# A GRU, attention, RK4 and FFN kernel: other stages for the FFN's side work on ScalarE and VectorE

## The chip, the cores and the metric

One core of a Trainium2 chip runs the whole program. The metric is the device time of one execution in microseconds: 1735.76 us before the change, the median of 3 runs (1735.63 to 1736.38).

## What is computed

Cut to what matters (x is 32 x 64 x 512, fp32):

```python
x = x + attn(gru(cond, x))                 # over 32 sequences of 64 steps
# the state q of the RK4 recurrence, 64 steps of 4 stages
def derivative(q, p, drive):
    dq = q - q ** 3 / 3.0 - p + drive + tanh(q) @ coupling.T + bias
    dp = EPSILON * (q + ALPHA - BETA * p)
    return dq, dp
# one step: dq1..dq4 from q, q + 0.5*DT*dq1, q + 0.5*DT*dq2, q + DT*dq3; then clip
# the FFN on every q, quantized to fp8 (scales per row from the row's maximum):
qx = fp8(xr / (max|xr| / 448))
g = qlinear(qx, w_gate); u = qlinear(qx, w_up)      # 512 -> 1408
t = silu(g) * u
y = qlinear(fp8(t / (max|t| / 448)), w_down)        # 1408 -> 512
out = x + y
```

The derivatives of a step follow each other: each stage needs the tanh of the state that the stage before it left. The FFN only reads the states.

## The kernel before

The program runs three parts one after the other: the GRU with the preparation of the FFN's weights, the attention, and the RK4 recurrence with the FFN. The change lies in the third, which takes the last 650 us or so. Every engine runs a program of its own, in order, and waits on semaphores.

**Groups and stages.** 64 time steps make 16 groups of 4 steps; a group has 16 stages, numbered k = 0 to 15 (k // 4 is the step, k % 4 the stage `st` of the RK4 step). Groups 0 to 2 and 15 are written out, groups 3 to 14 are the 12 turns of a loop (`in_groups`). A tile of the FFN is the 128 rows that a group of 4 steps has produced. Its work takes the three groups that follow: in group g, `tile(0)` is tile g-1, `tile(1)` is g-2 and `tile(2)` is g-3. After group 15 three groups without stages (16 to 18) finish the tiles that are left.

**One stage, engine by engine** (`stage` of each engine). DVE computes the new state with L1317 (from PSUM, where PE has summed) and turns it with two transposes (L1275). ACT squares the state (L956, into PSUM) and takes the tanh in two halves (L964), in stages with `st` = 0 the tanh first; then it weighs it for the p sum (L959). PE multiplies the tanh by the coupling in 32 products (L775) and mixes in the states for the next stage (L765). DVE meanwhile computes `ebuf` from the square (L1308), seeds the bank of the next stage (L1296, or L1294 after stages with `st` = 3), and then runs `fill()`, which is the FFN's slot of that stage, before it waits for PE and computes the next state. POOL adds the parts of p (`p_step`, L514 to L524) and then runs its own slot.

**The slots.** `slot(k, ...)` of PE, ACT, DVE and POOL place the FFN's work behind the stage k of its engine. On DVE before the change: the maximum of x (L1341, 512 wide) in k = 5 and its scale and reciprocal (L1346, L1347) in 6; x's exponents (L1350, L1351) in 7; `gate_part` (L1414) in 12, 13, 0 and 2; `gated_part` (L1422) in 14, 1, 4 and 5; the maximum of t in two halves of 704 (L1365) in 3 and 6, and its reciprocal (L1369 to L1371) in 7; t's exponents `t_bits` (L1395: 768 wide in 8, 640 in 9); `t_grid` (L1401) in 9 and 10; `t_added` (L1407) in 11 and 15; y's scaling (L1389) in 10. On ACT: Silu (`silu_part`, L978) in 12, 13, 0 and 2, the scaling of x (L1002) in 6, of t (`t_scaled`, L985) in 7 and 8, copies of transposed t (`t_kept`, L992) in 1 and 4, of x (L1005) in 10. On POOL, which the change doesn't touch: x's rounding (L543 in 7, L548 in 8), `gate_scaled` (L529) in 13, 14, 1 and 3, `t_rounded` (L536) in 12 and 15, and the output's sum (L563) in 11.

**The drive sum.** `drive_sum` (L1285) adds the drive of the next time step and the bias, both in SBUF, into PSUM. It stands behind `fill()` in the stages with `st` = 2, so in k = 2, 6, 10 and 14:

```python
                fill()
                if st == 2 and not end:
                    drive_sum(t + 1, (s + 1) % 4, g + 1 + (s == 3))
                dve.wait_ge(rk_e, n + 1)
                dve.wait_ge(rk_mm, n + 1)
```

Of the kernel before, what the change touches and what calls it, by code (L numbers as in the profile page):

```python
# [5 lines left out]
ALU = mybir.AluOpType  # L6
# [79 lines left out]
GROUP_STEPS = 12  # L86
# [51 lines left out]
def gru_attn_rk4_ffn(nc, xT, x, cond_quad, cond_T, W_ih, W_hh, bias_ih, bias_hh, sel, gamma, Wq, Wkv, Wo,  # L138
                     couplingT, bias_quad, w_gate, w_up, w_down, down_idx, ident, mean_of, trig, mask,
                     x1_scr, q_scr, wgu_scr, wd_scr, scale_scr, out):  # L140
    with ExitStack() as ctx:
# [123 lines left out]
        tam2 = f32(w.take(2), 2)  # L265
        tam, tsx, tsy, trs, xam, xsx, xrs = (f32(w.take(1), 1) for _ in range(7))
# [590 lines left out]
        def _(act):  # L857
# [137 lines left out]
            def slot(k, tile):  # L995
                i = tile(0)
                if i is not None:
                    if k == 6:
                        act.wait_ge(f_rq, i + 1)

                        wait_if(act, f_q8, i)
                        act.activation(vq, qt, ACT.Copy, scale=xrs).then_inc(f_vq, 1)  # L1002
                    if k == 10:
                        act.wait_ge(f_qT, i + 1)
                        act.activation(qxT, ps[:, 6, 0:2 * P].bitcast(BF16).rearrange("p (c n) -> p c n", c=NC), ACT.Copy).then_inc(f_qTcp, 1)  # L1005
                    if k in (12, 13):
                        silu_part(i, k - 12)
                i = tile(1)
                if i is not None:
                    if k in (0, 2):  # L1010
                        silu_part(i, 2 + k // 2)
                    if k in (7, 8):
                        t_scaled(i, k - 7)
                i = tile(2)
                if i is not None:
                    if k == 1:
                        t_kept(i, 0)
                    if k == 4:
                        t_kept(i, 1)

            act.wait_ge(ct_ld, 16 * 4)
            act.wait_ge(rk_bits, 1)
# [10 lines left out]
        def _(dve):  # L1033
# [267 lines left out]
            def stage(g, s, st, last, fill):  # L1301
# [10 lines left out]
                if st == 2 and not end:  # L1312
                    drive_sum(t + 1, (s + 1) % 4, g + 1 + (s == 3))
# [18 lines left out]
            def slot(v, k, tile):  # L1332
# [5 lines left out]
                if i is not None:  # L1338
                    if k == 5:
                        dve.wait_ge(q_ld, 16 * TILE_T * (i + 1))  # L1340
                        v.did(dve.tensor_reduce(xam, qt, AX.X, ALU.max, apply_absolute_value=True))  # L1341
                    if k == 6:
                        v.need(v.n)
                        if tile(1) is not None:
                            dve.wait_ge(f_gated, GU_T * tile(1) + GU_T)
                        v.need(v.did(dve.tensor_scalar(xsx, xam, 1.0 / FP8_MAX, None, ALU.mult)))  # L1346
                        dve.reciprocal(xrs, xsx).then_inc(f_rq, 1)  # L1347
                    if k == 7:
                        dve.wait_ge(f_vq, PRIMED + i + 1)
                        v.need(v.did(dve.tensor_scalar(eq.bitcast(U32), vq.bitcast(U32), EXP_BITS, None, ALU.bitwise_and)))  # L1350
                        dve.tensor_scalar(eq, eq, FP8_TINY, ROUND_AT, ALU.max, ALU.mult).then_inc(f_xe, 1)  # L1351
                    if k in (12, 13):
                        gate_part(i, k - 12)
# [3 lines left out]
                if i is not None:  # L1357
# [4 lines left out]
                    if k in (3, 6):  # L1362
                        half = k // 6
                        dve.wait_ge(f_gated, GU_T * i + 2 * half + 2)
                        v.did(dve.tensor_reduce(tam2[:, half:half + 1], tt[:, half * 2 * GU_N:(half + 1) * 2 * GU_N], AX.X, ALU.max,  # L1365
                                                apply_absolute_value=True))
                    if k == 7:
                        v.need(v.n)
                        v.need(v.did(dve.tensor_reduce(tam, tam2, AX.X, ALU.max)))  # L1369
# [148 lines left out]
```

## Time and profile before

| | us |
|---|---|
| median of 3 runs (lowest, highest) | 1735.76 (1735.63, 1736.38) |
| the profiled execution, its own time | 1733.82 |
| its span in the profile | 1732.0 |
| PE busy (matmuls) | 1551.0 (90%) |
| DVE busy | 1126.0 (65%) |
| ACT busy | 507.8 (29%) |
| POOL busy | 380.3 (22%) |
| first and last state update L1317 | 1079.8 and 1686.1 |

Times in the profile are counted from the span's start. In the timeline a row is one instruction (or a few alike in a row), with its start and its length; in brackets stands how long its engine had been idle before it and which instruction released it. A row without brackets followed its engine's earlier work directly. An engine starts an instruction a little before the one ahead of it has ended. `mem` is SBUF and `ps` is PSUM, so `ps<-mem` is an instruction whose inputs are all in SBUF and whose output is in PSUM.

### The profile page before, as it was taken

Reading aid. Unit: us, or ns where it says so; the run is one execution under the profiler, and the core shown is the slowest. Engines: PE = TensorE matmul, PEld = TensorE weight load, DVE = VectorE, ACT = ScalarE, POOL = GpSimd, SP = SyncE. Lnnn points to the kernel's source line nnn. Section 1 sums busy time; section 2 is a strip of 40 time slices with the busy share of each in tenths; the row PEclk is TensorE's granted clock in tenths of the full one; section 3 lists DMA queues with packets and bytes.
Section 4 is the critical chain, followed back from the end, with each engine's and each line's share of the span. In section 5 each row is a group of like instructions: output and inputs, shape, how many; then the busy total and the mean of one; then the engine's idle time right before and its main releaser. Section 6 shows DMA issues by size and latency. Waiting matters only on the chain.

```text
span 1732.0 us, 45724 instructions
## 1 busy us (share of the span) xinstructions
PE 1551.0 (90%) x16744; PEld 951.5 (55%) x16744; DVE 1126.0 (65%) x3319; ACT 507.8 (29%) x1589; POOL 380.3 (22%) x554
## 2 busy tenths in 40 slices
PE   5999899999859999999999998788888888888884
PEld 2333333333738576675767753556666666666662
DVE  2888743333786475664747541568888888888885
ACT  1233211112120202102020110355555555555552
POOL 1222010000000000000000000235555555555554
PEclk9999999999969999999999998999999999999997
DMA  7322210005000000000000005101111111111111
GB/s 303 79 76 61 79 29 12 12 11 111 1 0 1 25 0 24 6 18 23 1 24 0 24 6 184 42 23 29 33 31 44 35 35 33 30 33 30 42 35 35
DMA packets 88432, 70.27 MB, mean 41 GB/s; under 512 B 30728, under 2 KB 80824, under 8 KB 87352
## 3 DMA queue, kind: packets, MB, share of 16 engines
q1 hardware_dynamic: 86616, 63.75, 12.7%
q0 software_dynamic: 1760, 5.77, 1.2%
q8 instruction: 35, 0.57, 0.1%
q14 instruction: 21, 0.17, 0.0%
HBM read 52.55 MB, written 16.92 MB: 40 GB/s over the span
## 4 chain that ended last, share of the span: by engine, by line
PE 69%; DVE 14%; issue 8%; ACT 5%; DMA 2%; POOL 1%; SPq 1%; ACTq 0%; DVEq 0%; POOLq 0%
PE ps L681 13%; PE ps L671 13%; PE ps L775 10%; PE ps L588 9%; PE ps L596 9%; PE ps L715 3%; PE ps L765 2%; PE ps L739 2%; ACT mem L964 2%; DVE mem L1317 2%; DVE mem L1275 2%; ACT ps L956 2%; PE ps L692 1%; PE ps L789 1%; PE ps L585 1%
## 5 line engine op out<-in xcount | busy, mean ns | idle before, releaser
L775 PE MATMUL ps<-mem 128*32 128x128 f32 x8192 | 280.7, 278 | 89.7 <-ACT mem L964 85.6
L775 PEld LDWEIGHTS ps<-mem 128*32 128x32 f32 x8192 | 212.8, 111 | 165.2 <-ACT mem L964 118.3
L671 PE MATMUL ps<-mem 128*128 128x512 f32 x512 | 224.6, 593 | 0.0
L681 PE MATMUL ps<-mem 128*128 128x256 f32 x1024 | 222.3, 379 | 0.0
L681 PEld LDWEIGHTS ps<-mem 128*128 128x128 f32 x1024 | 194.2, 190 | 25.8
L514 POOL TENSOR_TENSOR mem<-mem 128x128 f32<-128x128 f32 x64 | 30.7, 480 | 784.7 <-ACT mem L959 784.5
L588 PE MATMUL ps<-mem 128*32 128x384 f32 x2048 | 181.5, 496 | 0.0
L596 PE MATMUL ps<-mem 128*32 128x384 f32 x2048 | 179.0, 491 | 2.7 <-DVE mem L1122 2.7
L671 PEld LDWEIGHTS ps<-mem 128*128 128x128 f32 x512 | 95.7, 190 | 109.6 <-issue 109.2
L518 POOL TENSOR_TENSOR mem<-mem 128x128 f32<-128x128 f32 x192 | 101.2, 527 | 171.8 <-ACT mem L959 165.7
L765 PE MATMUL ps<-mem 128*128 128x128 f32 x768 | 138.6, 304 | 0.0
L964 ACT ACTIVATE mem<-mem 128x64 f32<-128x64 f32 x512 | 102.0, 246 | 111.6 <-DVE mem L1275 111.6
L931 ACT ACTIVATE mem<-mem 128x512 f32<-128x512 f32 x32 | 19.7, 630 | 391.3 <-DVE mem L1216 391.3
L596 PEld LDWEIGHTS ps<-mem 128*32 128x32 f32 x2048 | 67.0, 111 | 103.1 <-issue 87.0
L765 PEld LDWEIGHTS ps<-mem 128*128 128x128 f32 x768 | 101.5, 192 | 38.8 <-issue 26.7
L1108 DVE TENSOR_TENSOR mem<-mem,ps 128x128 f32<-128x128 f32 x64 | 18.4, 287 | 158.9 <-ACT mem L860 158.8
L1179 DVE TENSOR_TENSOR mem<-ps,mem 64x256 f32<-64x256 f32 x272 | 114.7, 422 | 8.4
L588 PEld LDWEIGHTS ps<-mem 128*32 128x32 f32 x2048 | 60.7, 111 | 90.3 <-issue 90.3
L956 ACT ACTIVATE ps<-mem 128x128 f32<-128x128 f32 x256 | 71.0, 277 | 125.6 <-DVE mem L1317 119.6
L1308 DVE SCALAR_TENSOR_TENSOR mem<-ps,mem 128x128 f32<-128x128 f32 x256 | 74.5, 291 | 42.8 <-ACT ps L956 42.3
L789 PE MATMUL ps<-mem 128*128 128x352 bf16 x512 | 98.8, 318 | 2.7 <-DVE mem L1422 1.1
L1177 DVE TENSOR_TENSOR mem<-ps,mem 128x256 f32<-128x256 f32 x136 | 57.7, 425 | 66.9 <-PE ps L692 37.1
(129 smaller groups left out, 2104.8 us busy)
## 6 DMA issues: line engine op xcount, KB each, us to landing
mem<-x_scr SPq DMA_DIRECT2D x128, 64.0 KB, 1.8
mem<-in_xT SPq DMA_DIRECT2D x64, 64.0 KB, 1.8
mem<-in_Wq SPq DMA_DIRECT2D x1, 4096.0 KB
mem<-in_Wo SPq DMA_DIRECT2D x1, 4096.0 KB
mem<-in_x SPq DMA_DIRECT2D x16, 256.0 KB, 2.7
x_scr<-mem SPq DMA_DIRECT2D x32, 128.0 KB, 2.3
q_scr<-mem SPq DMA_DIRECT2D x64, 64.0 KB, 1.6
mem<-q_scr SPq DMA_DIRECT2D x64, 64.0 KB, 1.9
```

What stands on the lines that cost most here:

```text
L518: tt(pacc, pacc, pw[1 + st], ALU.add).then_inc(rk_pa, 1)
L588: mm = pe.matmul(ps[32 * j:32 * j + 32, par, 0:3 * P].rearrange("p (g n) -> p g n", g=3), xt[par][:, c, :], wih[:, c, :].rearrange("p (g j ...
L596: mm = pe.matmul(ps[32 * j:32 * j + 32, par, P:4 * P].rearrange("p (g n) -> p g n", g=3), hT[1 - par][:, c, :], whh[:, c, :].rearrange("p ...
L671: mm = pe.matmul(ps[:, 6 + pr, :], aoT[:, h, pr * P:pr * P + P], wo[:, h, :], start=(h == 0), stop=(h == HEADS - 1))
L681: mm = pe.matmul(ps[:, h % Q_BANKS, 0:BLK], wq[:, c, h * DH:(h + 1) * DH], xnb[:, c, :], start=(c == 0), stop=(c == NC - 1))
L765: pe.matmul(ps[:, st % 2, 0:P], mix[m], (None, qn[(s - 1) % 4], *qst)[k], start=False, stop=False, skip_group_check=True)
L775: mm = pe.matmul(ps[32 * j:32 * j + 32, st % 2, 0:P], thT[:, c, :], ct[:, c, j * P:(j + 1) * P], start=False, stop=(c == NC - 1), skip_gro ...
L789: mm = pe.matmul(ps[:, 2 + order % 2, 0:GU_N], qxT[:, c, :], (wgT if gate else wuT)[:, c, m * GU_N:(m + 1) * GU_N], start=(c == 0), stop=( ...
L956: act.activation(ps[:, 5, 0:P], src, ACT.Square, scale=(STEP[st] / 3) ** 0.5).then_inc(rk_sq, 1)
L964: act.activation(thT[:, 2 * half:2 * half + 2, :], qsT[:, 2 * half:2 * half + 2, :], ACT.Tanh).then_inc(rk_th, 1)
L1179: dve.tensor_tensor(share[b:b + DH // 2], src[a:a + DH // 2], bcast(trigs[:, tr + 1, :], BLK_B)[a:a + DH // 2], ALU.mult).then_inc(done, 1)
L1308: stt(out=ebuf, in0=ps[:, 5, 0:P], scalar=KEPT[st], in1=qs, op0=ALU.subtract, op1=ALU.mult).then_inc(rk_e, 1)
```

## The change

Nothing is computed otherwise, except that t's maximum is taken in four parts in place of two, and a copy of x's scale is added. In the stages of a group:

- ACT: Silu goes from k = 12, 13, 0, 2 to 13, 14, 1, 3; x's scaling from 6 to 4; the copies of transposed t from 1 and 4 to 0 and 5.
- DVE: x's maximum, scale and reciprocal go to k = 3, the scale into `xnew`, which is copied to `xsx` in 8. t's maximum is taken in parts of 352 in k = 1, 2, 5 and 6, and its reciprocal goes from 7 to 6.
- DVE: the drive sum goes from the stages with `st` = 2 to those with `st` = 0, so from k = 2, 6, 10, 14 to 0, 4, 8, 12.
- ACT: two waits ahead of the first group are dropped; DVE gets one wait on its own earlier work in k = 12.

```diff
--- before.py
+++ after.py
@@ -83,7 +83,7 @@
 GU_SLOTS = (11, 12, 13, 15, 0, 1, 3, 4)
 DOWN_SLOTS = (5, 7, 8, 9)
 T_PARTS = ((0, 6 * P), (6 * P, INNER))
-GROUP_STEPS = 12
+GROUP_STEPS = 15
 
 
 def wait_if(eng, sem, value):
@@ -262,8 +262,8 @@
         t8T = bf16(w.take(INNER // 2), IC, P)
         ysc = f32(w.take(D), D)
         yout = f32(w.take(D), D)
-        tam2 = f32(w.take(2), 2)
-        tam, tsx, tsy, trs, xam, xsx, xrs = (f32(w.take(1), 1) for _ in range(7))
+        tam4 = f32(w.take(4), 4)
+        tam, tsx, tsy, trs, xam, xnew, xsx, xrs = (f32(w.take(1), 1) for _ in range(8))
 
         (wih_ld, whh_ld, w_att, b_ld, c_ld, xt_ld0, xt_ld1, h0_ld, st_ld, wg_ld, wu_ld, idx_ld, wd_ld, x_ld, x1_wr, q_ld, x1_ld,
          o_wr, ct_ld) = (sem(n) for n in (
@@ -995,7 +995,7 @@
             def slot(k, tile):
                 i = tile(0)
                 if i is not None:
-                    if k == 6:
+                    if k == 4:
                         act.wait_ge(f_rq, i + 1)
 
                         wait_if(act, f_q8, i)
@@ -1003,23 +1003,20 @@
                     if k == 10:
                         act.wait_ge(f_qT, i + 1)
                         act.activation(qxT, ps[:, 6, 0:2 * P].bitcast(BF16).rearrange("p (c n) -> p c n", c=NC), ACT.Copy).then_inc(f_qTcp, 1)
-                    if k in (12, 13):
-                        silu_part(i, k - 12)
+                    if k in (13, 14):
+                        silu_part(i, k - 13)
                 i = tile(1)
                 if i is not None:
-                    if k in (0, 2):
+                    if k in (1, 3):
                         silu_part(i, 2 + k // 2)
                     if k in (7, 8):
                         t_scaled(i, k - 7)
                 i = tile(2)
                 if i is not None:
-                    if k == 1:
+                    if k == 0:
                         t_kept(i, 0)
-                    if k == 4:
+                    if k == 5:
                         t_kept(i, 1)
-
-            act.wait_ge(ct_ld, 16 * 4)
-            act.wait_ge(rk_bits, 1)
 
             def group(g, rk, tile):
                 for k in range(16):
@@ -1309,7 +1306,7 @@
                 if st < 3:
                     seed(t, s, st + 1)
                 fill()
-                if st == 2 and not end:
+                if st == 0 and not (last and s == 3):
                     drive_sum(t + 1, (s + 1) % 4, g + 1 + (s == 3))
                 dve.wait_ge(rk_e, n + 1)
                 dve.wait_ge(rk_mm, n + 1)
@@ -1336,20 +1333,22 @@
                     v.did(dve.tensor_copy(tsy, tsx))
                 i = tile(0)
                 if i is not None:
-                    if k == 5:
+                    if k == 3:
                         dve.wait_ge(q_ld, 16 * TILE_T * (i + 1))
-                        v.did(dve.tensor_reduce(xam, qt, AX.X, ALU.max, apply_absolute_value=True))
-                    if k == 6:
-                        v.need(v.n)
-                        if tile(1) is not None:
-                            dve.wait_ge(f_gated, GU_T * tile(1) + GU_T)
-                        v.need(v.did(dve.tensor_scalar(xsx, xam, 1.0 / FP8_MAX, None, ALU.mult)))
-                        dve.reciprocal(xrs, xsx).then_inc(f_rq, 1)
+                        v.need(v.did(dve.tensor_reduce(xam, qt, AX.X, ALU.max, apply_absolute_value=True)))
+                        v.need(v.did(dve.tensor_scalar(xnew, xam, 1.0 / FP8_MAX, None, ALU.mult)))
+                        dve.reciprocal(xrs, xnew).then_inc(f_rq, 1)
                     if k == 7:
                         dve.wait_ge(f_vq, PRIMED + i + 1)
                         v.need(v.did(dve.tensor_scalar(eq.bitcast(U32), vq.bitcast(U32), EXP_BITS, None, ALU.bitwise_and)))
                         dve.tensor_scalar(eq, eq, FP8_TINY, ROUND_AT, ALU.max, ALU.mult).then_inc(f_xe, 1)
+                    if k == 8:
+                        if tile(1) is not None:
+                            dve.wait_ge(f_gated, GU_T * tile(1) + GU_T)
+                        v.did(dve.tensor_copy(xsx, xnew))
                     if k in (12, 13):
+                        if k == 12:
+                            v.need(v.n)
                         gate_part(i, k - 12)
                     if k == 14:
                         gated_part(i, 0)
@@ -1359,14 +1358,13 @@
                         gate_part(i, 2 + k // 2)
                     if k in (1, 4, 5):
                         gated_part(i, {1: 1, 4: 2, 5: 3}[k])
-                    if k in (3, 6):
-                        half = k // 6
-                        dve.wait_ge(f_gated, GU_T * i + 2 * half + 2)
-                        v.did(dve.tensor_reduce(tam2[:, half:half + 1], tt[:, half * 2 * GU_N:(half + 1) * 2 * GU_N], AX.X, ALU.max,
-                                                apply_absolute_value=True))
-                    if k == 7:
+                    if k in (1, 2, 5, 6):
+                        m = (1, 2, 5, 6).index(k)
+                        dve.wait_ge(f_gated, GU_T * i + m + 1)
+                        v.did(dve.tensor_reduce(tam4[:, m:m + 1], tt[:, m * GU_N:(m + 1) * GU_N], AX.X, ALU.max, apply_absolute_value=True))
+                    if k == 6:
                         v.need(v.n)
-                        v.need(v.did(dve.tensor_reduce(tam, tam2, AX.X, ALU.max)))
+                        v.need(v.did(dve.tensor_reduce(tam, tam4, AX.X, ALU.max)))
                         v.need(v.did(dve.tensor_scalar(tsx, tam, 1.0 / FP8_MAX, None, ALU.mult)))
                         dve.reciprocal(trs, tsx).then_inc(f_rt, 1)
                     if k == 8:
```

PE's and POOL's instructions stand in the same order as before; only line numbers differ. Two places on DVE, both inside the loop over groups 3 to 14. The lines are shifted there: L1317 is L1314 in the changed kernel, L1308 is L1305, L1296 is L1293, L1285 is L1282, L1395 is L1393, L1414 is L1412.

The stage k = 8, before (from `ebuf` to the new state; ISA and REGISTER_ALU rows compute the values of later waits):

```order
L1308 SCALAR_TENSOR_TENSOR mem<-ps,mem 128x128 [waits rk_sq]
L1296 SCALAR_TENSOR_TENSOR ps<-mem,ps 128x128
L1394 ISA
L1395 TENSOR_SCALAR mem<-mem 128x768 [waits f_vt]
L1317 SCALAR_TENSOR_TENSOR mem<-ps,mem 128x128 [waits rk_mm,rk_e]
```

and with the change (L1348 is the copy of x's scale):

```order
L1305 SCALAR_TENSOR_TENSOR mem<-ps,mem 128x128 [waits rk_sq]
L1293 SCALAR_TENSOR_TENSOR ps<-mem,ps 128x128
L1348 COPY mem<-mem 128x1 [waits f_gated]
L1392 ISA
L1393 TENSOR_SCALAR mem<-mem 128x768 [waits f_vt]
L1282 TENSOR_TENSOR ps<-mem 128x128 [waits drive_ld3]
L1314 SCALAR_TENSOR_TENSOR mem<-ps,mem 128x128 [waits rk_mm,rk_e]
```

Two instructions are new there: the copy ahead of `t_bits`, and the drive sum behind it, ahead of the new state.

The stage k = 12, before (L1414 is `gate_part`):

```order
L1308 SCALAR_TENSOR_TENSOR mem<-ps,mem 128x128 [waits rk_sq]
L1296 SCALAR_TENSOR_TENSOR ps<-mem,ps 128x128
L1411 ISA
L92 REGISTER_ALU [waits f_g]
L1414 SCALAR_TENSOR_TENSOR mem<-ps,mem 128x352 [waits f_sig]
L1317 SCALAR_TENSOR_TENSOR mem<-ps,mem 128x128 [waits rk_mm,rk_e]
```

and with the change:

```order
L1305 SCALAR_TENSOR_TENSOR mem<-ps,mem 128x128 [waits rk_sq]
L1293 SCALAR_TENSOR_TENSOR ps<-mem,ps 128x128
L1409 ISA [waits rk_v]
L92 REGISTER_ALU [waits f_g]
L1412 SCALAR_TENSOR_TENSOR mem<-ps,mem 128x352 [waits f_sig]
L1281 ISA
L1282 TENSOR_TENSOR ps<-mem 128x128 [waits drive_ld0]
L1314 SCALAR_TENSOR_TENSOR mem<-ps,mem 128x128 [waits rk_mm,rk_e]
```

The drive sum now stands between `gate_part` and the new state. The stages 0 and 4 get it at the same place.

## Rows read from the trace of the kernel before

**Rows 1.** The page, part 4: the chain that ended last, by engine
```profile
PE 69%; DVE 14%; issue 8%; ACT 5%; DMA 2%; POOL 1%; SPq 1%; ACTq 0%; DVEq 0%; POOLq 0%
```

**Rows 2.** Timeline, DVE, stages 2 and 3: start, length, engine, line, operation
```profile
1312.50 0.29 DVE L1317 SCALAR_TENSOR_TENSOR mem<-ps,mem 128x128 f32<-128x128 f32 x1 [0.27 <-PE ps L775]
1313.35 0.88 DVE L1365 TENSOR_REDUCE mem<-mem 128x1 f32<-128x704 f32 x1
1314.63 0.30 DVE L1317 SCALAR_TENSOR_TENSOR ps<-ps,mem 128x128 f32<-128x128 f32 x1 [0.41 <-PE ps L775]
```

**Rows 3.** Timeline, DVE, ACT and POOL, stages 7 and 8
```profile
1323.54 0.30 DVE L1317 SCALAR_TENSOR_TENSOR ps<-ps,mem 128x128 f32<-128x128 f32 x1
...
1323.70 0.94 ACT L985 ACTIVATE mem<-mem 128x768 f32<-128x768 f32 x1 [1.08 <-DVE mem L1371]
...
1324.04 1.27 POOL L543 TENSOR_TENSOR mem<-mem 128x512 f32<-128x512 f32 x1
...
1325.47 1.27 POOL L548 TENSOR_TENSOR mem<-mem 128x512 bf16<-128x512 f32 x1 [0.16 <-POOL mem L543]
...
1325.53 1.63 DVE L1395 TENSOR_SCALAR mem<-mem 128x768 uint32<-128x768 uint32 x1
...
1327.08 0.28 DVE L1317 SCALAR_TENSOR_TENSOR mem<-ps,mem 128x128 f32<-128x128 f32 x1
```

**Rows 4.** Timeline, DVE and SP, from stage 15 into stage 0
```profile
1305.62 0.30 DVE L1317 SCALAR_TENSOR_TENSOR ps<-ps,mem 128x128 f32<-128x128 f32 x1 [0.47 <-PE ps L775]
...
1307.45 0.58 DVE L1414 SCALAR_TENSOR_TENSOR mem<-ps,mem 128x352 f32<-128x352 f32 x1
...
1308.04 1.75 SPq L435 DMA_DIRECT2D mem<-q_scr  x4
```

**Rows 5.** Timeline, DVE, ACT and POOL, stages 11 to 13
```profile
1334.56 0.30 DVE L1317 SCALAR_TENSOR_TENSOR ps<-ps,mem 128x128 f32<-128x128 f32 x1 [0.25 <-PE ps L775]
...
1336.45 1.82 POOL L536 TENSOR_TENSOR mem<-mem 128x768 bf16<-128x768 f32 x1
...
1336.48 0.58 DVE L1414 SCALAR_TENSOR_TENSOR mem<-ps,mem 128x352 f32<-128x352 f32 x1
...
1336.97 0.28 DVE L1317 SCALAR_TENSOR_TENSOR mem<-ps,mem 128x128 f32<-128x128 f32 x1
...
1337.17 0.50 ACT L978 ACTIVATE mem<-mem 128x352 f32<-128x352 f32 x1 [0.90 <-DVE mem L1414]
...
1339.29 0.29 DVE L1317 SCALAR_TENSOR_TENSOR mem<-ps,mem 128x128 f32<-128x128 f32 x1 [0.44 <-PE ps L775]
```

**Rows 6.** Timeline, DVE and POOL: two places with the drive sum L1285
```profile
1178.15 0.56 POOL L518 TENSOR_TENSOR mem<-mem 128x128 f32<-128x128 f32 x1 [0.93 <-ACT mem L959]
...
1178.32 0.55 DVE L1285 TENSOR_TENSOR ps<-mem 128x128 f32<-128x128 f32 x1
...
1331.46 0.29 DVE L1285 TENSOR_TENSOR ps<-mem 128x128 f32<-128x128 f32 x1
...
1331.66 0.28 DVE L1317 SCALAR_TENSOR_TENSOR mem<-ps,mem 128x128 f32<-128x128 f32 x1
```

**Rows 7.** Timeline, DVE and POOL, after the last stage
```profile
1715.30 2.75 DVE L1407 TENSOR_TENSOR mem<-mem 128x768 f32<-128x768 f32 x2
...
1715.46 1.90 POOL L563 TENSOR_TENSOR mem<-mem 128x512 f32<-128x512 f32 x1 [6.39 <-DVE mem L1389]
```

**Rows 8.** Timeline, DVE and POOL, stage 7 in groups 2 and 6
```profile
1170.65 0.46 POOL L518 TENSOR_TENSOR mem<-mem 128x128 f32<-128x128 f32 x1 [1.82 <-ACT mem L959]
...
1170.66 0.73 DVE L1351 TENSOR_SCALAR mem<-mem 128x512 f32<-128x512 f32 x1
...
1322.71 0.43 DVE L1351 TENSOR_SCALAR mem<-mem 128x512 f32<-128x512 f32 x1
...
1322.77 0.68 POOL L518 TENSOR_TENSOR mem<-mem 128x128 f32<-128x128 f32 x1 [1.82 <-ACT mem L959]
```

**Rows 9.** Timeline, DVE, after the last stage: the loads of the last tile
```profile
1690.66 0.69 DVE L1341 TENSOR_REDUCE mem<-mem 128x1 f32<-128x512 f32 x1 [0.45 <-DMA mem<-q_scr]
```

## The prediction

> **What bounds the kernel now.** I read four views: the chain that ended last, the timeline of each engine through one turn of the loop, the timelines of places where DVE and POOL meet, and the end behind the last stage. The change touches the RK4 part alone, and there a stage costs what lies between two state updates L1317. The shortest are 2.13 us: from 1312.50 to 1314.63 in [rows 2], where DVE did a maximum of 0.88 us on the side and still waited 0.41 us for PE. So side work is free as long as it fits behind DVE's own part. PE has 69% of the chain [rows 1], mostly as a link of this ring (tanh, product, update, transpose). Two of the stages that the change touches are longer because something ends late.
>
> From stage 7 to 8 it is 3.54 us (1323.54 to 1327.08) [rows 3]. ACT's scaling of t starts only at 1323.70, when its reciprocal is there, and keeps ACT from the tanh. And t's exponents L1395, 768 wide, take 1.63 us: they start 0.06 us behind POOL's L548, which lasts 1.27 us, and end 0.42 us after it. DVE and POOL hold each other up here.
>
> From 11 to 12 it is 2.41 us and from 12 to 13 2.32 us [rows 5]. In stage 12 `gate_part` ends what DVE has to do and L1317 follows without idle time; then Silu (1337.17 to 1337.67) keeps ACT from the square of the new state.
>
> **Who holds whom.** Rows 6 to 8 are about instructions of DVE that read two SBUF operands, or read and write wide ones in SBUF, beside POOL's. The drive sum takes 0.29 us alone and the next instruction starts 0.20 us after it [rows 6]. Where POOL's L518 was under way until 1178.71, it took 0.55 and ended at 1178.87, so 0.16 behind POOL. Behind the last stage [rows 7] two L1407 stand back to back; POOL's L563 starts 0.16 us after the first, takes 1.90 in place of the 1.27 of sums of its size [rows 3], and the second L1407 ends 0.68 us after L563. So a waiting POOL gets its turn between two DVE instructions, and the second one waits for all of POOL's. In [rows 8] L1351 starts 0.01 us behind POOL's L518 and takes 0.73; where it starts 0.06 ahead it takes 0.43 and L518 pays (0.68).
>
> **The change, per turn of the loop** (12 turns, groups 3 to 14):
>
> 1. Silu one stage later: it starts right behind ACT's own work and is over before the next state. The stages 12 and 0 lose what is above the floor: 2.32 less some 2.15, -0.17 each, -0.34 (bounds 0, if something else ends as late, and -0.38 by the 2.13 of [rows 2]). In 13, 14, 1 and 3 a Silu of 0.50 us lies in ACT's idle time.
> 2. The drive sum in stages 0, 4 and 12: DVE has no idle time ahead of L1317 there, and behind `gate_part` or `gated_part` the sum adds its 0.20 us to each. Stages 0 and 4: +0.40.
> 3. In stage 12 it meets POOL's `t_rounded`. The sum would start at 1336.97 and run into L536, which holds POOL from 1336.45 to 1338.27 [rows 5]. By [rows 6] it ends 0.16 behind it, at 1338.43, and L1317 starts 0.09 before that end (0.20 after the start of a 0.29 one), at 1338.34 in place of 1336.97: **+1.36**. L536 doesn't move, since POOL's row of work ahead of it is the same. Bounds: +0.20 if the sum isn't held, +1.45 if L1317 waits for its end.
> 4. The drive sum leaves 2, 6, 10 and 14. In 2 and 14 it was hidden. In 10 L1317 comes 0.20 earlier (1331.46 to 1331.66), but the tanh behind it waits for ACT's copy of x, which hangs on PE: 0. In 6 L1317 gets back to PE's pace: -0.03.
> 5. Maxima: 0.88 us for 704 [rows 2] and 0.69 for 512 [rows 9] make some 0.5 for 352, an estimate. In 1, 2 and 5 this fits ahead of the update by 0.1 us or more, in 6 with the three small ones (0.15 to 0.16 us each, 0.19 apart) by 0.2. x's maximum in 3 takes the place of t's, with two small ones behind it. It needs the tile's loads 4.4 us earlier than in 5; their last is issued by 1309.8 [rows 4] and stage 3's slot starts at 1313.35 [rows 2]: hidden. All 0. Should 1 or 5 miss by 0.05, a turn costs 0.1 more.
> 6. Reciprocal of t in 6, so ACT scales t (0.94) right behind its own work of stage 7, beside PE's product, and is done before the new state of 1323.54; the tanh comes in time. x's scaling in 4 and the copies of t in 0 and 5 lie in ACT's idle time in the same way: 0, and 0.1 each if one should reach the next square. The start of L1395 moves from 1.99 behind L1317 (1323.54 to 1325.53) to 1.84 as in stage 0 [rows 4], plus 0.06 for the copy ahead: 1.90. POOL's L548 stays at 1.93 behind, with L543 over at 1.77 [rows 3]. **L1395 is first by 0.03 us.** It then runs its 0.56, and L548 gets POOL's turn behind it and ends at some 3.59. But the drive sum is the next on DVE, and as the second L1407 of [rows 7] it waits for L548: end 3.74, L1317 at 3.65 in place of 3.54. +0.11. If L548 is first, L1395 ends where it did and the sum adds +0.20. The gain of this move (L1317 at 2.58, so -0.96) is there only if the sum slips in behind L1395.
>
> Sum of a turn: -0.34 + 0.40 + 1.36 - 0.03 + 0.11 = **+1.50**, times 12 is +18.0. Group 1: its stage 8 has no L1395, but the sum meets L548 (+0.6). Group 2: about +0.5, since L536 is over in time there. Group 15: +1.6, as a turn. Together +2.7. Behind the last stage DVE waits for the last tile's loads until 1690.66 [rows 9]; two gated parts and t's maxima of the tile before stand behind this wait now, and the last tile's chain starts about 1 us later, of which a shorter queue later gives back some: +0.8, between -0.4 and +2. In all **+21.5** on 1733.82, the profiled execution's own time (1.8 above its span); the median of the runs stands 1.9 above it, so 1735.76 + 21.5 = **1757.3 us**, 1.2% slower.
>
> Which of the two is first in stage 8 is worth 0.09 a turn. The rows leave it open: POOL wins from 0.01 ahead, DVE from 0.06 ahead, and 0.03 lies between. [...]
>
> **Rivals.**
> - *The sum slips in behind L1395* before POOL takes its turn: stage 8 gives 1.07 less, a turn +0.43, the whole 12 x 0.43 + 2.7 + 0.8 = +8.7, 1744.5 us. For it: L1395 is another instruction than L1407, and the next one starts 0.08 before it ends. Against it: [rows 7]. 7 in 100.
> - *Faster: the drive sum isn't held by L548 and L536.* Then stage 12 costs 0.20 and stage 8 gives 0.96: -0.34 + 0.60 - 0.03 - 0.96 = -0.73 a turn, -8.8 for the loop; with groups 1, 2 and 15 (+1.0) and the end (+0.8) -7.0, 1728.8 us. It decides at stage 12: with stage 8's 0.96 won, the change pays from where the sum costs less than about 0.8 there. Against it speak the 0.55 us and [rows 7]; for it only that no row shows the sum beside L536. 7 in 100.
> - *Held at stage 8 alone*: 1.16 less a turn than forecast, and as much in group 15: some +6.4, 1742.2 us. 4 in 100.
> - *Little happens*: ACT and DVE have more room than the rows show and the parts cancel, within 0.2%. 4 in 100.
>
> **The numbers.** The forecast has 78 in 100. Its own range is 1754.5 to 1761: 0.05 a turn at stage 12, 0.1 at stages 1 and 5, 1.1 for the lost lead, -1.2 to +1.2 for the end. To leave out no more than 2 in 10 the range reaches to the first rival: 1744 to 1762. A change of 0.2% (3.5 us) is about what a measurement of this kernel can tell from none. Faster by more 7 in 100, within it 4, slower 89.
>
> **What would show it.** In the changed profile the drive sum of stage 12 (L1282) lasts about 1.45 us and ends 0.16 behind POOL's L536; stage 11 to 12 takes 3.8 us. In stage 8 L1393 takes 0.56, L548 1.65 by its row, and the drive sum 1.36. If L1393 takes 1.7, L548 was first. Stages 12 to 13 and 0 to 1 take 2.14, 15 to 0 and 3 to 4 2.53. Wrong would be a drive sum of 0.29 us in stage 12 with L536 under way, a tile load that holds x's maximum in stage 3 (any idle time ahead of it that ends with a DMA), or a stage 1, 2, 5 or 6 longer than before.

## The result and the profile after

| | before | after |
|---|---|---|
| median of 4 runs (lowest, highest) | 1735.70 (1734.32, 1736.38) | 1755.76 (1755.51, 1756.66) |
| span of the profiled execution | 1732.0 | 1753.9 |
| one turn of the loop (groups 3 to 14) | 38.05 | 39.53 |

The ratio is 1.0118, with a 95% interval of 1.01 to 1.0135: slower, by 20.06 us (the two profiled executions differ by 21.9, of which 1.3 lies ahead of the first state update). The state update is now L1314 (L1317 before), the drive sum L1282 (L1285), t's exponents L1393 (L1395), the gate's scaling L1412 (L1414).

The page of the changed kernel, parts 1 and 4:
```profile
PE 1546.9 (88%) x16703; PEld 949.5 (54%) x16744; DVE 1148.1 (65%) x3367; ACT 508.2 (29%) x1589; POOL 384.1 (22%) x554
...
PE 69%; DVE 14%; issue 6%; ACT 5%; DMA 2%; POOL 2%; SPq 1%; DVEq 0%; POOLq 0%; ACTq 0%
```
The shares by engine are nearly those of [rows 1]. DVE is 22 us longer busy. The groups of instructions by line and shape, from 1173 to 1690 us (busy, mean ns of one), say which instruction that is. Before:
```profile
L1395 DVE TENSOR_SCALAR mem<-mem 128x768 uint32<-128x768 uint32 x14 | 21.7, 1550 | 0.0
L548 POOL TENSOR_TENSOR mem<-mem 128x512 bf16<-128x512 f32 x14 | 17.8, 1274 | 2.1 <-POOL mem L543 1.9
L1285 DVE TENSOR_TENSOR ps<-mem 128x128 f32<-128x128 f32 x53 | 16.8, 316 | 0.0
```
After:
```profile
L1282 DVE TENSOR_TENSOR ps<-mem 128x128 f32<-128x128 f32 x52 | 41.7, 803 | 0.0
...
L548 POOL TENSOR_TENSOR mem<-mem 128x512 bf16<-128x512 f32 x14 | 22.2, 1585 | 2.1 <-POOL mem L543 1.9
...
L1393 DVE TENSOR_SCALAR mem<-mem 128x768 uint32<-128x768 uint32 x14 | 9.1, 652 | 0.0
```
The exponents gave back 12.6 us and the drive sum took 24.9. In stage 8 the exponents were 1.63 us long [rows 3] and now are 0.55, while the drive sum behind them is 1.36 long: DVE's stall moved from one instruction to the other. In stage 12 the sum is 1.44 long, and that hold is new. The sum alone takes 0.29 (once more at both places in e3), so in these rows some 1.07 and 1.15 us of the sum's length are time in which it is held, and the 41.7 us count them as busy.

Where that is on the path, from the timelines (start, length). Stage 8, DVE and POOL, to be set beside [rows 3]; the update that opens it stands at 1330.97:
```profile
1331.47 1.27 POOL L543 TENSOR_TENSOR mem<-mem 128x512 f32<-128x512 f32 x1
...
1332.88 0.55 DVE L1393 TENSOR_SCALAR mem<-mem 128x768 uint32<-128x768 uint32 x1
1332.90 1.65 POOL L548 TENSOR_TENSOR mem<-mem 128x512 bf16<-128x512 f32 x1 [0.16 <-POOL mem L543]
...
1333.34 1.36 DVE L1282 TENSOR_TENSOR ps<-mem 128x128 f32<-128x128 f32 x1
...
1334.62 0.28 DVE L1314 SCALAR_TENSOR_TENSOR mem<-ps,mem 128x128 f32<-128x128 f32 x1
```
L1393 starts 0.02 us ahead of POOL and is done in a third of its old time. L548 pays 0.38, and the drive sum behind L1393 then waits for all of L548 and ends 0.15 behind it: 7 to 8 takes 3.65 in place of 3.54. Stage 12, to be set beside [rows 5]; its update stands at 1342.11:
```profile
1343.99 1.81 POOL L536 TENSOR_TENSOR mem<-mem 128x768 bf16<-128x768 f32 x1
1344.02 0.58 DVE L1412 SCALAR_TENSOR_TENSOR mem<-ps,mem 128x352 f32<-128x352 f32 x1
...
1344.52 1.44 DVE L1282 TENSOR_TENSOR ps<-mem 128x128 f32<-128x128 f32 x1
...
1345.87 0.28 DVE L1314 SCALAR_TENSOR_TENSOR mem<-ps,mem 128x128 f32<-128x128 f32 x1
```
The sum ends 0.16 behind L536, and 11 to 12 takes 3.77 in place of 2.41.

Mean stage lengths of the loop's turns in each kernel, from one update to the next (us). The nine stages that aren't listed differ by less than 0.1, but for the 0.2 of the drive sum in 3 to 4:

| kernel | 0-1 | 7-8 | 9-10 | 10-11 | 11-12 | 12-13 | 15-0 | turn | median |
|---|---|---|---|---|---|---|---|---|---|
| before | 2.31 | 3.54 | 2.41 | 2.90 | 2.41 | 2.31 | 2.33 | 38.05 | 1735.70 |
| changed | 2.12 | 3.65 | 2.22 | 3.10 | 3.77 | 2.12 | 2.53 | 39.53 | 1755.76 |
| e1 drive sum back | 2.12 | 2.37 | 2.41 | 2.90 | 2.41 | 2.12 | 2.33 | 36.53 | 1716.85 |
| e2 drive sum alone | 2.12 | 3.74 | 2.22 | 3.10 | 3.77 | 2.12 | 2.53 | 39.62 | 1755.05 |
| e3 bias in PSUM | 2.12 | 2.57 | 2.22 | 3.10 | 2.61 | 2.12 | 2.53 | 37.27 | 1728.20 |
| e4 e1, one copy ahead | 2.12 | 2.43 | 2.41 | 2.90 | 2.47 | 2.13 | 2.33 | 36.67 | 1720.40 |
| e5 e1, transposes early | 2.12 | 2.37 | 2.41 | 2.12 | 2.33 | 2.12 | 2.33 | 35.67 | 1704.84 |
| e6 e1, Silu back | 3.00 | 2.37 | 2.41 | 2.90 | 2.41 | 2.31 | 2.33 | 37.60 | 1731.63 |
| e7 e1, two copies ahead | 2.12 | 3.55 | 2.41 | 2.90 | 2.43 | 2.12 | 2.33 | 37.68 | 1731.87 |
| e8 e1, t's reciprocal back | 2.12 | 3.54 | 2.41 | 2.90 | 2.41 | 2.12 | 2.33 | 37.65 | 1732.22 |
| e9 e6, t's copies back | 2.31 | 2.37 | 2.41 | 2.90 | 2.41 | 2.31 | 2.33 | 36.93 | 1720.43 |
| e10 e5, copy behind | 2.12 | 2.37 | 2.42 | 2.12 | 2.33 | 2.12 | 2.33 | 35.65 | 1704.90 |

(For e4 the row leaves out the one turn told of below.)

### The profile page after: what moved, and what is told of

It reads as the page before. It is cut to its first block, busy times and chain, and to the rows that moved or that the text cites. A ratio compares the mean times of both kernels' runs of the same rounds, so it can differ in the third digit from the quotient of the medians.

```text
span 1753.9 us, 45716 instructions
## 1 busy us (share of the span) xinstructions
PE 1546.9 (88%) x16703; PEld 949.5 (54%) x16744; DVE 1148.1 (65%) x3367; ACT 508.2 (29%) x1589; POOL 384.1 (22%) x554
## 4 chain that ended last, share of the span: by engine, by line
PE 69%; DVE 14%; issue 6%; ACT 5%; DMA 2%; POOL 2%; SPq 1%; DVEq 0%; POOLq 0%; ACTq 0%
PE ps L681 13%; PE ps L671 13%; PE ps L775 11%; PE ps L588 9%; PE ps L596 8%; PE ps L715 3%; PE ps L765 3%; DVE ps L1282 3%; PE ps L739 2%; ACT mem L964 2%; DVE mem L1272 2%; ACT ps L956 2%; DVE mem L1314 2%; DMA mem<-in_xT 1%; PE ps L692 1%
## 5 line engine op out<-in xcount | busy, mean ns | idle before, releaser
L518 POOL TENSOR_TENSOR mem<-mem 128x128 f32<-128x128 f32 x192 | 101.1, 526 | 171.9 <-ACT mem L959 165.8
L956 ACT ACTIVATE ps<-mem 128x128 f32<-128x128 f32 x256 | 72.2, 282 | 198.9 <-DVE mem L1314 191.6
L485 POOL COPY mem<-mem 128x128 f32 (+1 forms) x64 | 31.4, 490 | 321.5 <-DVE mem L1119 321.5
```

The costliest lines, as they stand in the source:

```text
L518: tt(pacc, pacc, pw[1 + st], ALU.add).then_inc(rk_pa, 1)
L956: act.activation(ps[:, 5, 0:P], src, ACT.Square, scale=(STEP[st] / 3) ** 0.5).then_inc(rk_sq, 1)
```

## The experiments

**e1: the drive sum where it was, all else changed.**
```
-                if st == 0 and not (last and s == 3):
+                if st == 2 and not end:
                     drive_sum(t + 1, (s + 1) % 4, g + 1 + (s == 3))
```


> The changed kernel with one line undone: the drive sum stands in stages 2, 6, 10 and 14 again, all else as changed. Theory (the drive sum is all that costs; held by POOL in stages 8 and 12): against the changed kernel a turn loses 0.20 + 0.20 in stages 0 and 4, 1.36 in stage 12, and in stage 8 the 1.27 that L1314 waits for the sum (3.65 to about 2.38, since L1393 is still first by 0.02 to 0.04 us and takes 0.55): -3.0 a turn, -36 for 12 turns, some -5 for groups 1, 2 and 15. So 1715 to 1719 us, about 18 below the kernel before, of which 1.16 x 12 = 14 come from stage 7 to 8 and 0.38 x 12 = 4.5 from Silu. Rival (other parts of the change cost as well, or ACT's scaling sets stage 8 once DVE is out of the way): stage 7 to 8 stays at 3.1 or more and the time at 1728 or more.

1716.85 us, ratio to the kernel before 0.9904 (0.9883 to 0.9925). Stage 8 of its timeline:
```profile
1322.56 0.55 DVE L1393 TENSOR_SCALAR mem<-mem 128x768 uint32<-128x768 uint32 x1
1322.60 1.64 POOL L548 TENSOR_TENSOR mem<-mem 128x512 bf16<-128x512 f32 x1 [0.16 <-POOL mem L543]
...
1323.03 0.28 DVE L1314 SCALAR_TENSOR_TENSOR mem<-ps,mem 128x128 f32<-128x128 f32 x1
```
The next instruction on DVE is now L1314, which takes one operand from SBUF and one from PSUM, and it goes in 0.28 us while L548 runs. So one line of the change costs 39 us, and the rest gains 18 to 19 where the sum stays.

**e2: the kernel before with the drive sum alone moved.**
```
-                if st == 2 and not end:
+                if st == 0 and not (last and s == 3):
```


> The kernel before with the drive sum alone moved to stages 0, 4, 8 and 12. Theory: 0.20 in stages 0 and 4, 1.36 in stage 12 (sum 1.44 long, over 0.16 behind L536), 0.20 in stage 8 (L548 is first there as before, L1395 takes its 1.63, the sum follows it free of POOL), -0.03 in 6: +1.93 a turn, +23 for 12 turns, some +1.5 for groups 1 and 2: 1758 to 1762 us. Rival (the sum is held only where Silu and the moved reciprocals bring it there): 0.20 at each of four places, +9.6, about 1745 us.

1755.05 us, ratio 1.0121 (1.0101 to 1.0141), the changed kernel's time. The theory's holds are there (11 to 12 is 3.77 and 7 to 8 is 3.74, 0.20 more than before), but a turn costs 1.57 more than before and not 1.93. What is missing are stages 0 to 1 and 12 to 13, 0.19 each: they take 2.12 although Silu stands in its old slots. ACT in stage 12 of this kernel shows why; the update L1317 stands at 1344.68:
```profile
1343.51 0.50 ACT L978 ACTIVATE mem<-mem 128x352 f32<-128x352 f32 x1 [0.89 <-DVE mem L1414]
1344.99 0.28 ACT L956 ACTIVATE ps<-mem 128x128 f32<-128x128 f32 x1 [0.99 <-DVE mem L1317]
```
Silu waits for the gate's scaling and not for the update. Where the drive sum delays the update, Silu is over before it. So the 0.38 is won by either of the two and not by both, and beside the drive sum everything else in the change is worth 0.08 a turn.

**e3: the bias in PSUM.** The changed kernel, the sum in the same place:
```
+            biasp = ps[:, 4, 3 * P:4 * P]
-            dve.tensor_scalar(biasq, biasq, -ALPHA / BETA, None, ALU.add).then_inc(rk_start, 1)
+            dve.tensor_scalar(biasp, biasq, -ALPHA / BETA, None, ALU.add).then_inc(rk_start, 1)
...
-                dve.tensor_tensor(driven(s), drive[s], biasq, ALU.add).then_inc(rk_drive, 1)
+                dve.tensor_tensor(driven(s), drive[s], biasp, ALU.add).then_inc(rk_drive, 1)
```


> The changed kernel, but the bias that the drive sum adds lies in PSUM, so the sum reads one SBUF operand in place of two. Same place, same size, same order. Theory (two SBUF operands make the sum wait for POOL): in stage 12 it takes about 0.3 beside L536 and stage 11 to 12 takes 2.5 in place of 3.77; in stage 8 it takes 0.3 behind L1393 and stage 7 to 8 takes 2.6 in place of 3.65. That is -2.3 a turn, -28 in all: 1727 to 1730 us, below the kernel before. Rival (the place or the order of the sum costs, whatever it reads; or its SBUF output is enough to be held): stage 11 to 12 stays at 3.77, the time at 1754 to 1756.

1728.20 us, ratio 0.9965 (0.9954 to 0.9975). Stage 12, DVE and POOL:
```profile
1335.94 1.82 POOL L536 TENSOR_TENSOR mem<-mem 128x768 bf16<-128x768 f32 x1
1335.97 0.58 DVE L1413 SCALAR_TENSOR_TENSOR mem<-ps,mem 128x352 f32<-128x352 f32 x1
...
1336.46 0.29 DVE L1283 TENSOR_TENSOR ps<-mem,ps 128x128 f32<-128x128 f32 x1
...
1336.66 0.28 DVE L1315 SCALAR_TENSOR_TENSOR mem<-ps,mem 128x128 f32<-128x128 f32 x1
```
`ps<-mem` has become `ps<-mem,ps`, and the sum takes 0.29 in place of 1.44 with L536 under way. In stage 8, behind the exponents (L1394 here) and beside L548, it is the same:
```profile
1325.90 0.55 DVE L1394 TENSOR_SCALAR mem<-mem 128x768 uint32<-128x768 uint32 x1
1325.94 1.65 POOL L548 TENSOR_TENSOR mem<-mem 128x512 bf16<-128x512 f32 x1 [0.16 <-POOL mem L543]
...
1326.37 0.29 DVE L1283 TENSOR_TENSOR ps<-mem,ps 128x128 f32<-128x128 f32 x1
```
The sum's output lies in PSUM in every kernel here, so the expectation's "SBUF output" is nothing that it has. The sum's hold hangs on its second SBUF operand, and not on the place or the order: with one it takes 0.29 where with two it took 1.44 and 1.36. The place still has its own, small price: a turn is 0.74 longer than in e1, some 0.2 in each of the stages 0, 4, 8 and 12.

**e4 and e11: L1393 a little later.** e1 with one more copy of a single element (`pad` is one more f32 column) ahead of it. The added line shifts L1393 to L1394 here, and to L1395 in e7:
```
                         v.did(dve.tensor_copy(xsx, xnew))
+                        v.did(dve.tensor_copy(pad, xnew))
```


> As the run with the drive sum back, with one more copy of a single element on DVE ahead of L1393 in stage 8, so that L1393 starts some 0.06 us later and L548 is first by about 0.03 us. Theory (whoever starts first holds the other for its whole instruction): L1393 takes about 1.6 in place of 0.55 and stage 7 to 8 returns to 3.54: +1.1 a turn, 13 to 14 us above the run with the drive sum back, 1729 to 1733 us. Rival (DVE and POOL share, and the lead decides nothing): +0.06 a turn, under 1 us.

1720.40 us (1718.67 to 1721.82). Neither number came: it now started 0.012 to 0.029 us behind L548, and was still first in 11 turns of 12. The turn it lost and the one before it, in its timeline:
```profile
1539.45 1.27 POOL L548 TENSOR_TENSOR mem<-mem 128x512 bf16<-128x512 f32 x1 [0.16 <-POOL mem L543]
1539.48 1.66 DVE L1394 TENSOR_SCALAR mem<-mem 128x768 uint32<-128x768 uint32 x1
```
```profile
1502.82 1.70 POOL L548 TENSOR_TENSOR mem<-mem 128x512 bf16<-128x512 f32 x1 [0.16 <-POOL mem L543]
...
1502.84 0.55 DVE L1394 TENSOR_SCALAR mem<-mem 128x768 uint32<-128x768 uint32 x1
```
In the lost turn 7 to 8 took 3.54, in the others 2.43. The same kernel once more:

> The kernel with one more copy ahead of L1393, the same as before, for a second profile. Theory (at a lag of 0.02 to 0.03 us the race is decided turn by turn): some turns of 12 have stage 7 to 8 at 3.54 and L1393 at 1.66, the others 2.43 and 0.55, and the lost ones are those where L1393 starts 0.027 or more behind L548. Rival (the group decides, not the lag): group 12 again and only that.

1715.89 us, a single execution, so the time says little. All 12 turns were won, at lags of 0.020 to 0.029. So the rival falls, group 12 wasn't lost again, but a border at 0.027 doesn't stand either: at 0.029 two turns were won here and one was lost in e4. e4's median is 3.5 above e1's, of which the longer turns make 1.6 and each lost turn 1.1; how many were lost in its other executions isn't known.

**e7: two copies ahead.**
```
                         v.did(dve.tensor_copy(xsx, xnew))
+                        v.did(dve.tensor_copy(pad, xnew))
+                        v.did(dve.tensor_copy(pad2, xnew))
```


> As the run with one more copy of a single element ahead of L1393, with two. One copy moved the start to 1.96 behind the update, 0.012 to 0.029 behind POOL's L548, and DVE still was first in 11 turns of 12; it lost at 0.029. Theory (a race by start, whose border lies 0.03 us behind POOL's start): with two copies it starts at 2.02, 0.08 behind, loses in all 12 turns, takes 1.6, and stage 7 to 8 takes 3.6: 1731 to 1734 us. Rival (L1393 is first for another reason than its start, e.g. because ACT no longer has its scaling beside it): stage 7 to 8 2.5 in nearly all turns, 1718 to 1720.

1731.87 us, ratio 0.9979 (0.9969 to 0.9989). The exponents start 0.073 to 0.091 behind and lose all 12 turns, at 1.60 to 1.61 us; 7 to 8 takes 3.55. Some 0.06 us of start, the time of one copy, are worth 11 us. Over all 13 profiles, this instruction of DVE was first in every turn in which it started up to 0.028 us behind L548, went both ways at 0.029, and lost from 0.048 on; no turn lies between. Behind the last stage it lost at 0.028, 0.030 and 0.033.

**e8: the last step of t's maximum and its reciprocal in stage 7 again.**
```
-                    if k == 6:
+                    if k == 7:
                         v.need(v.n)
                         v.need(v.did(dve.tensor_reduce(tam, tam4, AX.X, ALU.max)))
```


> As the run with the drive sum back, but the last three instructions of t's maximum and its reciprocal stand in stage 7 again, the four partial maxima stay where the change put them. Theory (the reciprocal in 6 lets ACT scale t in time, and that alone brings L1393 to 1.90 and ahead of POOL): ACT scales t at the new state of stage 7 again, L1393 starts at 2.0 or later, L548 is first, 7 to 8 returns to 3.5 to 3.6: +1.2 a turn, +14: 1730 to 1733 us. Rival (the parts of the maximum, or x's moved reciprocal, bring it): 7 to 8 stays at 2.4 to 2.7 and the time at 1717 to 1720.

1732.22 us, ratio 0.9978 (0.9967 to 0.9989), a turn 1.12 longer than in e1, from 7 to 8 (3.54, +1.17), where L1393 starts 0.12 behind POOL: the 0.05 to 0.06 of the kernel before and the 0.06 of the copy ahead of it. So the parts of the maximum and x's move don't bring it forward, and the reciprocal's move is needed; no run made that move by itself.

**e6: Silu in its old slots, the rest as in e1.**
```
-                    if k in (13, 14):
-                        silu_part(i, k - 13)
+                    if k in (12, 13):
+                        silu_part(i, k - 12)
...
-                    if k in (1, 3):
+                    if k in (0, 2):
```


> As the run with the drive sum back, with Silu in its old stages 12, 13, 0 and 2. Theory (Silu is worth 0.19 in each of stages 12 and 0): 12 to 13 and 0 to 1 return to 2.31, +0.38 a turn, +4.6: 1721 to 1722 us. Rival (the drive sum of stage 0 or DVE's own length sets these stages once the rest has moved): no change, 1717.

1731.63 us, 10 above the theory. 12 to 13 went to 2.31 as expected, but 0 to 1 to 3.00. ACT there, with the update of stage 0 at 1344.78:
```profile
1344.98 0.50 ACT L978 ACTIVATE mem<-mem 128x352 f32<-128x352 f32 x1 [0.90 <-DVE mem L1412]
1345.38 0.79 ACT L992 ACTIVATE mem<-ps 128x768 bf16<-128x768 bf16 x1
1346.07 0.27 ACT L956 ACTIVATE ps<-mem 128x128 f32<-128x128 f32 x1
```
The change had moved ACT's copy of t, L992, into stage 0, and with Silu back there the next state's square L956 stands behind both. The expectation left that out.

**e9: e6, and t's copies back in 1 and 4.**
```
-                    if k == 0:
+                    if k == 1:
                         t_kept(i, 0)
-                    if k == 5:
+                    if k == 4:
                         t_kept(i, 1)
```


> The run with Silu back came out at 1731.6: stage 0 to 1 grew to 3.00, because ACT's copy of t, which the change moved from stage 1 to 0, stands behind Silu there (0.50 + 0.79 in a row). This kernel puts the copies of t back in 1 and 4 as well. Theory: 0 to 1 falls to the 2.31 of before and 12 to 13 stays at 2.31: +0.38 a turn above the run with the drive sum back, 1721 to 1722 us. Rival (Silu in stage 0 costs more than before for another reason, e.g. the maximum in stage 1 or t's new place in line): stage 0 to 1 stays at 2.5 or more, 1724 or more.

1720.43 us (1719.22 to 1725.34): a turn 0.40 longer than e1's, with 2.31 in both stages. So Silu's move is worth 0.38 a turn where the drive sum stands in its old place, and t's copy could go to stage 0 only because Silu left it.

**e5: PE's transposes of x's codes in stage 9.** e1 with
```
-                    if k == 10:
+                    if k == 9:
                         pe.wait_ge(f_q8, i + 1)
```


> As the run with the drive sum back, with PE's transposes of x's codes in stage 9 in place of 10, so that ACT's copy of them in stage 10 finds them ready. Theory (stage 10 to 11, 2.90, hangs on ACT's copy, which waits for PE behind its product, and the tanh waits behind the copy): 10 to 11 falls to 2.2 or so, -0.7 a turn, -8 to -9 for the loop: 1707 to 1710 us. Rival (ACT's copy itself or DVE's side work sets the stage): -0.2 a turn or less, 1714 or more.

1704.84 us, ratio 0.9828 (0.9803 to 0.9853). In e1 ACT's copy stands 1.91 us and waits for the transposes L810, which are behind PE's product, and the square L956 of the new state stands behind the copy:
```profile
1328.35 0.60 ACT L1005 ACTIVATE mem<-ps 128x512 bf16<-128x512 bf16 x1 [1.91 <-PE ps L810]
1328.84 0.28 ACT L956 ACTIVATE ps<-mem 128x128 f32<-128x128 f32 x1
```
In e5 it finds them done:
```profile
1321.09 0.58 ACT L1005 ACTIVATE mem<-ps 128x512 bf16<-128x512 bf16 x1
1322.72 0.28 ACT L956 ACTIVATE ps<-mem 128x128 f32<-128x128 f32 x1 [1.06 <-DVE mem L1314]
```
10 to 11 falls from 2.90 to 2.12, and 11 to 12 by 0.08.

**e10: e5 with the copy of x's scale behind L1393 in stage 8.**
```
-                    if k == 8:
-                        if tile(1) is not None:
-                            dve.wait_ge(f_gated, GU_T * tile(1) + GU_T)
-                        v.did(dve.tensor_copy(xsx, xnew))
...
                    if k == 15:
                        t_added(v, 1)
+                if tile(0) is not None and k == 8:
+                    if tile(1) is not None:
+                        dve.wait_ge(f_gated, GU_T * tile(1) + GU_T)
+                    v.did(dve.tensor_copy(xsx, xnew))
```


> As the run with the transposes early, with the copy of x's scale in stage 8 behind L1393 in place of ahead of it. Theory: L1393 starts at 1.84 behind the update in place of 1.90, 0.1 ahead of L548 in place of 0.035, a wider lead in the race, and DVE ends as early as before or as much as the copy earlier; stage 7 to 8 is 2.31 to 2.37, the time 1704 to 1705 us, within 1 us of the run with the transposes early. Rival (the copy of one element is held by L548 behind L1393, as the drive sum is): stage 7 to 8 rises to 3.6, the time to 1719.

1704.90 us, ratio 0.9826 (0.981 to 0.9843). Its stage 8:
```profile
1316.89 0.56 DVE L1393 TENSOR_SCALAR mem<-mem 128x768 uint32<-128x768 uint32 x1
...
1316.98 1.59 POOL L548 TENSOR_TENSOR mem<-mem 128x512 bf16<-128x512 f32 x1 [0.16 <-POOL mem L543]
...
1317.36 0.15 DVE L1380 COPY mem<-mem 128x1 f32<-128x1 f32 x1
1317.42 0.28 DVE L1314 SCALAR_TENSOR_TENSOR mem<-ps,mem 128x128 f32<-128x128 f32 x1
```
L1393 leads by 0.09 to 0.10 in every turn, and the copy of one element takes 0.15 us where the drive sum was held to 1.36. The time is e5's; what is gained is distance from the edge that e4 found. e5 and e10 are below both kernels of the case, by 31 us and 51 us.

## Why the prediction was right, and where it wasn't

Forecast 1757.3 us, 21.5 above the profiled execution; measured 1755.76, 20.06 above the median of the kernel before. By its own steps, from the updates of the two profiles:

| step | forecast | measured |
|---|---|---|
| Silu, stages 12 and 0 | -0.34 a turn | -0.38 |
| drive sum in 0 and 4 | +0.40 | +0.40 |
| drive sum in 12, behind L536 | +1.36 | +1.36 |
| stages 5 to 7 | -0.03 | -0.02 |
| stage 8 | +0.11 | +0.11 |
| stages 9 to 11 | 0 | +0.01 |
| a turn | +1.50 | +1.49 |
| group 1 | +0.6 | +0.24 |
| group 2 | +0.5 | +1.42 |
| group 15 | +1.6 | +0.34 |
| behind the last stage | +0.8 | +0.8 |

The total came nearer than its parts: group 2 and group 15 missed by +0.9 and -1.3, which nearly cancel, and that is luck. The 18 us of the loop are not: all 12 turns grew by 1.47 to 1.50. The steps measured add up to 20.6; the 1.3 us that the profiled execution lost ahead of the first update can't be told from chance, since that update stands anywhere from 1078.8 to 1082.0 in the runs whose code up to there is that of the changed kernel, and at 1079.8 before.

*The hold in stage 12* is right in mechanism (e3) and in size. [Rows 6] gave the end of a held sum, 0.16 behind POOL's, and L536's end did the rest.

*The order in stage 8* is right too: DVE starts 0.024 to 0.045 ahead of POOL in all 12 turns, where 0.03 was forecast, and L1393 takes 0.55 in all of them. That a lead of 0.03 is enough was the author's estimate: no row of before shows it. The sum then waits as the second L1407 of [rows 7] did. e1, e3 and e8 show each half: the reciprocal brings L1393 ahead of POOL (-1.17), the sum gives it back (+1.28). But the lead was not as thin as was written. The prediction put the border between 0.01 behind and 0.06 ahead, by [rows 8]; e4 puts it for L1393 against L548 at 0.03 behind. L1351 against L518 [rows 8] is another pair with another border: in the 13 profiles it lost all 39 times that it started 0.007 to 0.017 us behind, where L1393 won at 0.012 to 0.028. So rows of one pair don't tell the border of another.

*Stages 5 to 7* have the right sum by two errors. The -0.03 was for stage 6, by the drive sum's going, and e2 shows just that (2.27 to 2.24); but with the maxima and the small ones in it stage 6 takes 2.30, which the prediction had at 0 and had named as a sign of being wrong. Stage 5 fell by 0.05, since x's maximum left it (2.18 in e2, 2.12 in e1).

*Group 15* is the step that failed most. "Group 15: +1.6, as a turn" overlooks a condition of the diff: `not (last and s == 3)` puts no drive sum into stage 12 of the last group. There 11 to 12 stays at 2.33. What is left is 0.38 in 7 to 8, 0.20 in 3 to 4, and small terms of both signs.

*Groups 1 and 2* were off by -0.4 and +0.9, by TensorE's clock in the main. In stage 8 of group 1 the sum cost 0.59 as forecast, while 0 to 1 fell from 3.07 to 2.21 (its 32 products took 1.93 us before and 1.08 after; the granted clock from 1110 to 1125 was 0.89 before and 1.00 after). That hides some 0.6 that the forecast left out: 3 to 4 grew by 0.37, and 11 to 12 and 15 to 0 by 0.20 each, less 0.16 in 12 to 14. In group 2 it is 8 to 9 that takes 3.05 in place of 2.20: PE's 32 products need 1.93 us there and 1.08 in the stage before.
```profile
1174.16 1.08 PE L775 MATMUL ps<-mem 128*32 128x128 f32 x32 [1.14 <-ACT mem L964]
...
1177.43 1.93 PE L775 MATMUL ps<-mem 128*32 128x128 f32 x32 [1.77 <-ACT mem L964]
```
By windows, PEclk, the granted clock, is 0.91 on the mean from 1177 to 1197 and 1.00 behind it:
```profile
1177.00:1197.00 20.00, 17.18 (x309) 13.11 (x310) 14.38 (x52) 9.16 (x38) 10.42 (x14) 0.91 0.10 26
1197.00:1217.00 20.00, 16.83 (x311) 11.68 (x315) 17.77 (x68) 11.74 (x44) 9.19 (x14) 1.00 0.11 31
```
From 1177.3 to 1180.5 it is 0.50, and the product of 1.93 us lies in there; PE had stood idle for 1.77 us ahead of it. The change isn't shown to be the cause: in e9, with the drive sum in its old place, the same product took 1.90 after 1.56 idle, and in e3 it took 1.08 after 1.76. Such stages of 2.9 to 3.1, whose product takes 1.80 to 1.94 at a granted clock of 0.50 to 0.71, stand at one to four places in the first three groups of every profile of this study; only the very first has its fixed place.

*Behind the last stage* the step from the last update to the end grew by 0.75. That this is the forecast's +0.8 is luck, as far as the runs show. One kernel differs from itself by more: from the last update to the end e4 takes 47.65 and e11 46.52. And e1, with the same order behind the last stage, takes 46.06, against 45.88 before and 46.63 with the change, while e2, with the old order, takes 46.74. The mechanism named is that x's maximum of the last tile starts later. Now L1338, it starts 4.81 behind the last update (4.53 before, [rows 9]); the two gated parts and the maxima are done sooner than its loads come, and the wait for these has grown to 1.34:
```profile
1712.07 0.69 DVE L1338 TENSOR_REDUCE mem<-mem 128x1 f32<-128x512 f32 x1 [1.34 <-DMA mem<-q_scr]
```
So the start is 0.28 later and not 1, because the loads set it; what makes the rest of the 0.75 stays open.

*What the sum hid.* The terms add up, but Silu's -0.34 isn't earned by moving Silu here: e2 has it without that move. A prediction that priced Silu's move alone on top of the drive sum's would have been wrong by 0.38 a turn.

The three rivals that rest on an unheld sum are refuted by the rows above, which show it held in stage 8 and in stage 12, and the fourth by the time. e3 is what "the drive sum isn't held by L548 and L536" would have been: forecast 1728.8, measured with that hold taken away 1728.2.

## What to carry to other kernels

Before an instruction of DVE with two SBUF inputs is moved, look which of POOL's instructions is under way at its new place, and read what is left of it. Here that was the price within 0.15 us: the drive sum (0.29 alone, 1.44 held) paid 1.15 where 1.28 of L536 was left, and L1395 (0.55 as L1393, 1.63 held) 1.08 where 1.21 of L548 was left. One input kept in PSUM took the sum's price away (0.29 beside L536 in e3). Two SBUF inputs aren't the only case: L1395, now L1393, has one, 768 wide, and its output in SBUF, and besides being held to 1.63 it held L548 to 1.65 in place of 1.27 where it was first. Where DVE and POOL start within 0.1 us of each other, the order can be worth more than the instruction on DVE (1.17 us a turn in stage 8, where L1393 alone takes 0.55), so look what stands behind the winner as well, and keep the lead wide; and don't add the gains of two moves that clear the same stage.

## What was not expected of the hardware

- The border of the race isn't at equal starts as the profile records them, and it isn't the same for every pair: in the loop L1393 won at starts up to 0.028 us behind POOL's L548, while L1351 lost to L518 from 0.007 behind.
- A whole hold came or went by 0.06 us: 1.1 us a turn between e4 and e7.
- The end of a held instruction followed one sum in the three kinds measured, with DVE held as with POOL: it is the end of the one that holds, plus the held one's own length, less about 0.14 us. The drive sum (0.29 alone) ends 0.16 behind L536; L1395 (0.55 as L1393) ends 0.42 behind L548 [rows 3]; L548 (1.27) ends 1.13 behind L1393 in e1 (1324.24 against 1323.11). In the 13 profiles the 0.14 is 0.13 to 0.15 in each of these kinds. The rows don't tell whether the hold ends that much before the recorded end or whether that much of the held instruction goes on during it.
- A copy of one element from SBUF to SBUF ran beside L548 in 0.15 us (e10), right where the drive sum took 1.36.
